# Subtracting the row maxima of q on VectorE from PSUM to SBUF, in place of an identity product on TensorE

## The reference

```python
qh = einsum('bcn,oc->bon', layernorm(x), Wq)     # 512 = 8 heads x 64 rows
kh, vh = einsum('bcn,oc->bon', ctx, Wk), einsum('bcn,oc->bon', ctx, Wv)
qh = softmax(qh, axis=-2) * SCALE                # over the 64 rows of a head
kh = softmax(kh, axis=-1)                        # over the 1024 positions
context = einsum('bhdn,bhen->bhde', kh, vh)
out = einsum('bhde,bhdn->bhen', context, qh)
out = einsum('bcn,oc->bon', out, Wo) + bo        # then normalised by column, scaled
x = x + tanh(g_xattn) * out
```

## Time and profile before

| what | value |
|---|---|
| median of 3 runs | 1103.09 (1101.88 to 1105.66) |
| span of the profiled execution | 1101.1 |
| TensorE matmul busy | 1046.2 (95%) |
| VectorE busy | 702.1 (64%) |
| ScalarE busy | 510.1 (46%) |
| GpSimd busy | 419.3 (38%) |
| attention phase | from the start to about 650 |
| one full body in the steady part | 38.81 |

### The profile page before, as it was taken

The page is one execution under the profiler, slowest core; times in us unless marked ns, Lnnn a source line. Parts: engine busy times, 40 slices in busy tenths (PEclk is TensorE's granted clock), DMA queues, the critical chain, the costliest instruction groups (busy, mean ns, idle before and its releaser), DMA issues. The chain is left out here.

```text
span 1101.1 us, 17249 instructions
## 1 busy us (share of the span) xinstructions
PE 1046.2 (95%) x5732; PEld 880.6 (80%) x5732; DVE 702.1 (64%) x1522; ACT 510.1 (46%) x855; POOL 419.3 (38%) x294
## 2 busy tenths in 40 slices
PE   6899999999999999999999879999999999999997
PEld 4688888888888888888788767888888888888886
DVE  6887887878788787878877648444434443334321
ACT  5576568558656755856675535311112221111110
POOL 2656657655655765575566411000000110000000
PEclk9999999999999999999999978999999999999999
DMA  6002012201201210220110038111111111111000
GB/s 225 24 20 77 30 46 76 76 13 63 76 19 57 76 63 13 76 76 19 57 57 34 6 139 235 39 39 38 38 38 38 38 38 38 38 38 38 19 22 36
DMA packets 25705, 60.34 MB, mean 55 GB/s; under 512 B 2448, under 2 KB 12176, under 8 KB 25680
## 3 DMA queue, kind: packets, MB, share of 16 engines
q1 hardware_dynamic: 23376, 58.99, 15.5%
q10 hardware_dynamic: 2304, 1.05, 0.3%
HBM read 43.26 MB, written 16.78 MB: 55 GB/s over the span
## 5 line engine op out<-in xcount | busy, mean ns | idle before, releaser
L1079 POOL TENSOR_TENSOR yT_lo<-yf,yT_hi 128x512 fp32r<-128x512 f32 x32 | 40.8, 1296 | 354.8 <-ACT yT_hi L1236 354.8
L266 POOL TENSOR_TENSOR qe<-qe,qrec 128x1024 f32<-128x1024 f32 x64 | 121.2, 1905 | 96.5 <-DVE qrec L542 96.5
L547 DVE TENSOR_TENSOR qT_lo<-ps,qT_hi 128x512 fp32r<-128x512 f32 x128 | 82.5, 686 | 47.6 <-ACT qT_hi L384 47.2
L259 POOL TENSOR_TENSOR qhalf<-qe 128x512 f32<-128x512 f32 x64 | 82.1, 1283 | 72.4 <-ACT qe L377 72.4
L1226 ACT ACTIVATE yf<-ps 128x512 f32<-128x512 f32 x32 | 17.5, 595 | 189.4 <-PE ps L1119 189.4
L67 PE MATMUL ps<-aT_hi,yT_hi 128*128 128x512 f32 x256 | 103.0, 402 | 0.0
L67 PE MATMUL ps<-bT_hi,hT_hi 128*128 128x512 f32 x256 | 102.6, 401 | 0.0
L68 PE MATMUL ps<-bT_hi,hT_lo 128*128 128x512 f32 x256 | 101.2, 395 | 0.0
L69 PE MATMUL ps<-bT_lo,hT_hi 128*128 128x512 f32 x256 | 101.2, 395 | 0.0
L69 PE MATMUL ps<-aT_lo,yT_hi 128*128 128x512 f32 x256 | 101.1, 395 | 0.0
L68 PE MATMUL ps<-aT_hi,yT_lo 128*128 128x512 f32 x256 | 101.1, 395 | 0.0
(11 more groups left out here) (159 smaller groups left out, 2628.3 us busy)
## 6 DMA issues: line engine op xcount, KB each, us to landing
ctx_in<-in_ctx SPq DMA_DIRECT2D x16, 512.0 KB, 3.3
x_in<-in_x SPq DMA_DIRECT2D x16, 512.0 KB, 3.2
x_res<-in_x SPq DMA_DIRECT2D x16, 512.0 KB, 3.7
x_scratch<-x SPq DMA_DIRECT2D x16, 512.0 KB, 2.9
out<-b_stage SPq DMA_DIRECT2D x16, 512.0 KB, 2.9
stage<-in_L_ffn_A SPq DMA_DIRECT2D x8, 512.0 KB, 4.6
stage<-in_L_ffn_B SPq DMA_DIRECT2D x8, 512.0 KB, 6.8
stage<-x_scratch SPq DMA_DIRECT2D x8, 512.0 KB, 3.9
```

Of the source, the lines that this page charges most:

```text
L259: nc.gpsimd.tensor_tensor(qhalf[:, p % 2, :].rearrange("p (h d) -> p h d", d=DH // 2), v[:, :, 0:DH // 2], v[:, :, DH // 2:DH], ALU.add).t ...
L266: nc.gpsimd.tensor_tensor(v, v, w, ALU.mult).then_inc(q_norm, 1)
L547: nc.vector.tensor_tensor(qT[1][:, :, v], psT[:, h, :].rearrange("p (j n) -> p j n", n=P), qT[0][:, :, v].bitcast(f32), ALU.subtract).then ...
```

## The change

`qmax` now holds plain maxima, in f32 and not negated. `shift_q` moves from TensorE to VectorE: right behind each `max_q` it waits for that maximum, reads `psQ` and the broadcast `qmax`, and writes the difference into `qe[:, p]`. The wait for `q_T` moves with it. `exp_q` reads and writes `qe[:, p]` in place. `mm_q` waits for `q_shift` where it waited for `q_exp`. The identity products on TensorE go.

```diff
                 def exp_q(b, p):
                     act.wait_ge(q_shift, 4 * b + p + 1)
-                    if started(b):
-                        act.wait_ge(q_T, 8 * b + 2 * p - 6)
-                    nc.scalar.activation(qe[:, p, :].rearrange("p (a n) -> p a n", a=2), psQ,
-                                         ACT.Exp).then_inc(q_exp, 1)
+                    nc.scalar.activation(qe[:, p, :], qe[:, p, :], ACT.Exp).then_inc(q_exp, 1)
...
                 def max_q(b, p):
                     dve.wait_ge(q_mm, 4 * b + p + 1)
                     nc.vector.tensor_reduce(qmax[:, p % 2, :], psQ.rearrange("p a (h d) -> p (a h) d", d=DH),
-                                            axis=AX.X, op=ALU.max, negate=True).then_inc(q_max, 1)
+                                            axis=AX.X, op=ALU.max).then_inc(q_max, 1)
+
+                def shift_q(b, p):
+                    dve.wait_ge(q_max, 4 * b + p + 1)
+                    if started(b):
+                        dve.wait_ge(q_T, 8 * b + 2 * p - 6)
+                    nc.vector.tensor_tensor(qe[:, p, :].rearrange("p (h d) -> p h d", d=DH),
+                                            psQ.rearrange("p a (h d) -> p (a h) d", d=DH),
+                                            qmax[:, p % 2, :].unsqueeze(2).broadcast_to([P, 2 * H, DH]),
+                                            ALU.subtract).then_inc(q_shift, 1)
...
# in VectorE's body, each max_q(b, p) is followed by:
+                        shift_q(b, p)
...
                     if p > 0:
-                        pe.wait_ge(q_exp, 4 * b + p)
+                        pe.wait_ge(q_shift, 4 * b + p)
                     elif started(b):
-                        pe.wait_ge(q_exp, 4 * b)
+                        pe.wait_ge(q_shift, 4 * b)
...
-                def shift_q(b, p):
-
-                    pe.wait_ge(q_max, 4 * b + p + 1)
-                    for h in range(2):
-                        m = qmax[:, p % 2, h * H:h * H + H].unsqueeze(2).broadcast_to([P, H, DH])
-                        last = nc.tensor.matmul(psQ[:, h, :], ident_r[:, :], m, start=False, stop=True,
-                                                skip_group_check=True)
-                    last.then_inc(q_shift, 1)
```

More of the change, by code:

```diff
@@ L124, in flamingo_layer @@
             qe = sb("qe", [P, 4, 2 * HD])
-            qmax = sb("qmax", [P, 2, 2 * H], f32r)
+            qmax = sb("qmax", [P, 2, 2 * H])
             qhalf = sb("qhalf", [P, 2, 2 * H * DH // 2])
@@ L589, in body @@
                         max_q(b, 0)
+                        shift_q(b, 0)
                         max_k(b, 1)
@@ L621, in body @@
                         max_q(b, 1)
+                        shift_q(b, 1)
                         max_k(b, 2)
@@ L631, in body @@
                         max_q(b, 2)
+                        shift_q(b, 2)
                         lo_k(b, 1, 0)
@@ L662, in body @@
                         max_q(b, 3)
+                        shift_q(b, 3)
                         lo_k(b, 3, 0)
@@ L866, in body @@
                         mm_k(b, 1)
-                        shift_q(b, 0)
                     if tail and head:
@@ L880, in body @@
                     if head:
-                        shift_q(b, 1)
                         if not started(b):
@@ L891, in body @@
                         output(b - 1, 0, range(CH // 2, CH))
-                    if head:
-                        shift_q(b, 2)
                     if tail:
@@ L912, in body @@
                         square_norms(b - 1)
-                    if head:
-                        shift_q(b, 3)
                 pe.wait_ge(w_lo, 1)
```

## The result

The changed kernel takes 1159.73 us (median of 4 runs, 1158.22 to 1164.69) against 1102.49 before (4 runs, the three of the table above and one more, 1100.51 to 1105.66): ratio 1.0526, 95% interval 1.0504 to 1.0547. The direction is as forecast, the size is not: +57 where +34 was predicted. The time lies outside the forecast's own range (1128 to 1147) and just inside the end, 1160, of the wider one of 8 in 10. The span went from 1101.1 to 1157.3.

What follows compares the result with a forecast made beforehand. TensorE's work was taken to set the body of 38.81 us, with VectorE taking over after the change. 7.1 + 20.4 (twelve at 1.7) + 6.5 = +34 gave a span of 1135.1, so 1137 us; range 1128 to 1147, 8 in 10 1112 to 1160.

Steps and rivals of the forecast that it cites:

- What TensorE gives up: Four pairs of identity products (L740) per body leave TensorE: 1.81 us per body, 29.0 over 16 batches.
- What VectorE takes on: Four subtractions from PSUM to SBUF per body, 1.22 us each: 1.25 added per piece, 5.0 per body.
- VectorE busy about 80 us more: Sign expected in the changed kernel's profile: VectorE's busy time up about 80 us over the kernel.
- Step 1: Start of a body: max_q(b,0) and its subtraction fit VectorE's 2.55 us wait before L604, free; TensorE 0.43 ahead.
- Steps 2 and 3: Middle of a body: subtractions delay lo_k, TensorE waits about 1.6 us ahead of each of two tr_q, 2.1 late.
- Step 5: End of a body: piece 3's subtraction delays lo_k(b,3), context waits about 1.3 us, next spread 1.25 later.
- Step 6: Roots on VectorE: GpSimd starts later relative to L54 and L56, only some 0.5 us of blocking left, gain 1.6.
- the blocking stays: Rival: GpSimd's two instructions still meet L54 and L56 in full, 1.6 us of twelve bodies lost: 1156, chance 0.17.
- the clock: Rival: TensorE's new waits lower its clock once per body, 15 x 3 = 45 us more: 1182, chance 0.03.
- The wait ahead of the spread: TensorE's wait ahead of the spread (L823), 1.69 us before, was to go down to about 1.
- The sum of the edges: First and last bodies: +7.1 us up to the first spread, 3.3 and 3.2 (6.5) in bodies 15 and 16.

Runs made afterwards that it cites:

- e3: Changed kernel with only piece 0 subtracted on VectorE, pieces 1 to 3 keeping the identity product on TensorE: 1096.34 us.
- e4: Changed kernel with pieces 0 to 2 subtracted on VectorE, piece 3 keeping the identity product on TensorE: 1141.76 us.
- e5: Changed kernel with the subtractions of pieces 1 to 3 behind the lo_k that followed them, and hi_q(b-1,2) ahead of exp_q(b,1) on ScalarE: 1130.79 us.
- e7: Kernel before the change, with one more wait on GpSimd so that its two instructions start behind the roots: 1076.78 us.
- e1: Changed kernel with five unused products on TensorE ahead of context, in its wait for lo_k: 1141.37 us.
- e13: Changed kernel with only piece 3 subtracted on VectorE, pieces 0 to 2 keeping the identity product on TensorE: 1128.61 us.
- e14: Changed kernel with two unused products on TensorE between the squares and the wait ahead of context: 1148.28 us.
- e15: Changed kernel with two unused products on TensorE ahead of the squares: 1148.05 us.
- e2: Changed kernel with five unused products ahead of context and five more ahead of each of tr_q(b-1,2) and tr_q(b-1,3): 1143.35 us.
- e12: e5 with eight unused products on TensorE in the wait ahead of the spread: 1116.47 us.
- e8: e3 and e7 together: piece 0 alone subtracted on VectorE, GpSimd's two instructions behind the roots: 1073.77 us.
- e10: Changed kernel with piece 3 on TensorE, subtractions 1 and 2 behind lo_k, hi_q(b-1,2) ahead of exp_q(b,1), GpSimd's two instructions behind the roots: 1079.46 us.
- e11: e10 with lo_k(b,0) and lo_k(b,1) also ahead of max_q(b,1) and max_q(b,2) on VectorE: 1099.99 us.
- e6: Changed kernel with lo_k(b,3) ahead of max_q(b,3) and its subtraction in VectorE's list: 1187.45 us.

## Why the prediction was right and where it was wrong

- **What TensorE gives up** (1.81 per body): in line with e3, where one pair of 0.43 brought 38.8 down to 38.4.
- **What VectorE takes on** (1.22 each, 1.25 per piece): 1225 ns, right. The sign "VectorE busy about 80 us more" was not: it is 56.6, since the same forecast took the blocking away, and L54 and L56 together fell by 1.75 in each body. TensorE's busy time was to fall by 30 to 50 us and rose by 9, by the matmuls at half clock.
- **Step 1** (piece 0 free): shown by e3.
- **Steps 2 and 3** (waits of 1.6 and 1.6 ahead of `tr_q`, 2.1 late at the end): 1.49 and 1.28, and `max_q(b,3)` starts 336.96 - 304.95 = 32.0 after the spread instead of 347.10 - 317.24 = 29.9, so 2.1. Shown by e4 alone; with the subtractions behind `lo_k` (e5) only 0.3 of the two waits is left.
- **Step 5** (TensorE waits ahead of `context`): forecast 1.3, measured 1.36.
- **Step 6** (blocking relieved): L54 fell from 1.28 to 0.57, L56 from 1.21 to 0.17. From `max_q(b,3)` to the last root it is now 8.3 instead of 8.8, where +1.25 - 1.6 = -0.35 was forecast. That GpSimd causes the blocking was only read from coinciding times; e7 shows it. So the rival "the blocking stays", whose 1156 lies nearest to the measured time, did not come: that its number is near is a coincidence.
- **The step that failed** is the clock: the sum left it out, as a rival of chance 0.03. The forecast argued, from a window at the start with gaps and a clock of 1.00, that this kernel bears such gaps. It does bear them ahead of `tr_q` (e4), and not ahead of `context`: there the clock fell to 0.50 in each of the twelve full bodies, and a body is 1.2 us longer than the 40.5 forecast in two of three and 2.4 in the third, 1.6 on average. The rival's price of 3 per body was about twice that. The steps that gave each wait its length never asked what TensorE had run just before: the wait ahead of `context` follows sixteen one-column products.
- **The wait ahead of the spread** was to be about 1; in e1, without the fall, it is 0.16. The transpositions that take 1.25 instead of 1.04 fill a part of it. This did not change the body, whose length VectorE sets there.
- **The sum of the edges** was too small. Up to the first spread 7.1 was forecast and 9.6 measured. In body 0 TensorE waits 3.50 for `exp_k(0,2)`, behind the late `max_k`, which the estimate had lumped into 4.4. The clock may have a share: it is at half for 10.2 us there, in the kernel before never. e1, with 9.3, doesn't part the two, as it leaves the waits of body 0 unfilled and has the same 10.2; e7 has 6.8 at half there and is only 0.5 late. For bodies 15 and 16 it was 6.5 forecast, 9.6 measured; e1 has 7.6. The -2.4 behind the spread at 681.55 was not forecast. It goes with the clock of the drain: from the same spread to the end the changed kernel has 10.7 us at half and takes 475.8, e13 has 11.0 and takes 475.7, e1 17.1 and 477.9, the kernel before 20.5 and 478.1. Why the drains differ, no run shows.

The account of the 56.2 of span: 34 forecast, 19.0 more in the twelve full bodies, 2.5 more up to the first spread, 3.1 more in bodies 15 and 16, and -2.4 behind them. The forecast missed 22.2 of it. Filling the wait ahead of `context` takes 17.4 back (the span of e1 is 1139.9), and the twelve full bodies of e1 alone are 17.4 shorter. So the clock is most of what was missed.

The Trainium skill ("TensorE: Matmul & The Clock Gate", HAM oscillation) describes a kernel in which an idle gap in every pass of its loop lets the clock fall in every pass. This trace agrees in that the clock is at 0.50 in a part of every full body of the changed kernel; the page's gaps are of 3 to 5 us, and here waits of 1.36 were enough, so for this kernel the measurement decides.

What exactly decides between a stretch that lowers the clock and one that doesn't stays open: e14 and e15 bore out neither simple form, the neighbourhood or the idle time alone. The traces do narrow it. In e1, e2, e5 and e12 the clock fell in five bodies behind the one-column products with no wait of TensorE over 0.11, so idle time is not needed. In the seven kernels where two full products of L740 follow the squares and `context` does not wait (before, e3, e4, e7, e8, e10, e11), none of their 84 full bodies has a fall. Yet e14, with two full products in the same place and a wait of 0.79 behind them, has seven falls in twelve. And in e5 and e6 waits of 2.27 and 3.53 behind full products lowered it, where 1.69 at the same place did not.

## What to carry to other kernels

When an edit makes TensorE wait, ask what the engine runs just before the new wait, not only how long the wait is: here a wait of 1.36 behind sixteen one-column products cost each body another 1.2 or 2.4 us by the clock, and waits of 1.3 to 1.5 behind full products (e4) cost nothing beyond themselves. A run with the wait filled by unused products shows this at once. Before moving work to an engine with "slack", walk its list to the next instruction that another engine waits for; piece 0 was free, pieces 1 to 3 were not, though the slack by busy time was larger than the load. And look for tiny instructions with long durations: delaying an engine that blocks them was worth 2.3%, more than any form of the change itself.

## What was unexpected of the hardware

- The clock fell to 0.50 behind a single wait of 1.52 us that followed sixteen one-column products (e13), and stayed there for more than 6 us, while waits of 1.47, 1.27 and 1.69 in one body left it at 1.00 (e4).
- With the same instructions in every body, the fall came in some and not in others: 12 of 12, 7, 5 and 1 of 12 in the changed kernel, e14, e15 and e1. The one of e1 came while TensorE was busy for 3.00 of 3.00 us, behind sixteen one-column and five full products.
- VectorE instructions on 9 columns took 1.2 to 1.3 us beside a GpSimd instruction that reads SBUF and 0.17 without (e7). The Trainium skill ("SBUF — State Buffer", who interferes with whom) states that of a VectorE instruction in a two-port mode, which `tensor_scalar` can enter, and a GpSimd instruction, the one that issues first blocks the other fully. The trace agrees for L54 and L56: they end with GpSimd's instruction. That they run in such a mode no run here shows.
